# Routed expert results stored in sorted order and gathered by GpSimd, instead of scattered to their tokens

## The reference

```python
x = layernorm(x + self_attention(x))          # 16 heads of 8
x = layernorm(x + cross_attention(x, ctx))    # softmax over the heads
# the feed-forward part, per token:
shared  = gelu(x @ sW1 + sb1) @ sW2 + sb2                     # 512 hidden
weights = softmax(x @ gW + gb)                                # 15 experts
topv, topi = top_k(weights, 3)
routed  = sum over the 3 of  topv * (gelu(x @ rW1[e] + rb1[e]) @ rW2[e] + rb2[e])   # 256 hidden
x = layernorm(shared + routed + x)
```

## Time and profile before

| what | us |
| --- | --- |
| median of 3 runs | 286.7 |
| fastest and slowest of them | 285.6 and 286.87 |
| span of the profiled execution | 319.6 |
| PE, DVE, ACT, POOL busy in it | 241.1, 221.6, 192.2, 179.0 |
| its 62 scatters of results, its 48 scatters of rows | 62.7, 48.0 |

### The profile page before, as it was taken

The page is one execution under the profiler, slowest core; times in us unless marked ns, Lnnn a source line. Parts: engine busy times, 40 slices in busy tenths (PEclk is TensorE's granted clock), DMA queues, the critical chain, the costliest instruction groups (busy, mean ns, idle before and its releaser), DMA issues.

```text
span 319.6 us, 7117 instructions
## 1 busy us (share of the span) xinstructions
PE 241.1 (75%) x2283; PEld 179.8 (56%) x2283; DVE 221.6 (69%) x630; ACT 192.2 (60%) x423; POOL 179.0 (56%) x166
## 2 busy tenths in 40 slices
PE   6989989877988767996761299688868867785970
PEld 3676868655535434452451156586857757674960
DVE  6777999989999998998520497043444434856875
ACT  4697997549976976754470350344554546563665
POOL 6132755330666738985677467135656566665752
PEclk9999999999997998998978589799999999999778
DMA  7672830124000002952211133123132263354462
GB/s 218 217 213 46 181 128 2 37 67 133 2 0 2 0 4 62 378 215 49 86 58 50 44 101 108 41 61 101 53 99 76 75 187 90 91 168 123 150 185 90
DMA packets 38597, 31.89 MB, mean 100 GB/s; under 512 B 12864, under 2 KB 31552, under 8 KB 38432
## 3 DMA queue, kind: packets, MB, share of 16 engines
q1 hardware_dynamic: 34608, 23.90, 26.6%
q0 software_dynamic: 3520, 7.27, 6.7%
q10 hardware_dynamic: 432, 0.27, 0.3%
HBM read 19.95 MB, written 11.47 MB: 98 GB/s over the span
## 4 chain that ended last, share of the span: by engine, by line
PE 44%; DVE 27%; issue 14%; ACT 4%; another core or an unknown queue 4%; POOL 4%; DMA 1%; DVEq 0%; SPq 0%; ACTq 0%
PE psum L994 12%; PE psum L985 9%; PE psum L783 5%; DVE prob_sums L1496 4%; PE psum L763 4%; DVE maxes L1490 3%; PE psum L977 2%; PE psum L568 2%; DVE prob_sums L1410 2%; POOL x_srt L1986 2%; PE psum L585 1%; DMA xT<-x_t 1%; DVE turned_room L1421 1%; DVE maxes L1405 1%
## 5 line engine op out<-in xcount | busy, mean ns | idle before, releaser
L2047 POOL DMA_INDIRECT y_tok<-k_heads,y_rows x62 | 62.7, 1012 | 50.8 <-ACT k_heads L1327 34.4
L1319 ACT ACTIVATE k_heads<-psum,k_heads 128x128 f32<-128x128 f32 x124 | 38.7, 365 | 38.5 <-PE psum L985 33.6
L1986 POOL DMA_INDIRECT x_srt<-v_blocks,slot x48 | 48.0, 1000 | 21.3 <-issue 17.2
L994 PE MATMUL psum<-k_heads 128*128 128x128 f32 x248 | 42.4, 295 | 18.0 <-issue 12.1
L1823 DVE COPY k_heads<-psum 128x128 f32<-128x128 f32 x62 | 17.8, 289 | 48.9 <-PE psum L977 32.7
L994 PEld LDWEIGHTS psum<-k_heads 128*128 128x128 f32 x248 | 34.2, 200 | 21.9 <-issue 15.2
L985 PE MATMUL psum<-k_heads 128*128 128x128 f32 x248 | 40.6, 288 | 5.2 <-DVE k_heads L1823 4.2
L1963 POOL TENSOR_TENSOR k_heads<-k_heads,inv_sums 128x1024 f32<-128x1024 f32 x14 | 27.1, 1939 | 24.0 <-DVE inv_sums L1503 23.9
L985 PEld LDWEIGHTS psum<-k_heads 128*128 128x128 f32 x248 | 33.8, 198 | 8.5 <-DVE k_heads L1823 7.4
L1951 POOL TENSOR_TENSOR probs<-probs,inv_sums 128x512 f32<-128x512 f32 x16 | 16.8, 1050 | 28.9 <-DVE inv_sums L1415 28.7
L1327 ACT ACTIVATE k_heads<-psum,k_heads 128x128 f32<-128x128 f32 x62 | 22.9, 370 | 11.3 <-PE psum L994 9.1
(11 more groups left out here) (191 smaller groups left out, 530.1 us busy)
## 6 DMA issues: line engine op xcount, KB each, us to landing
expert_w<-e_w SPq DMA_DIRECT2D x1, 4369.0 KB
k_heads<-x_srt SPq DMA_DIRECT2D x62, 65.0 KB
q_heads<-y_tok SPq DMA_DIRECT2D x8, 256.0 KB
x_srt<-pad SPq DMA_DIRECT2D x16, 65.0 KB
xT<-x_t SPq DMA_DIRECT2D x4, 256.0 KB, 5.1
ctxT_k<-ctx_k SPq DMA_DIRECT2D x2, 512.0 KB, 5.5
v_scr<-v_rows SPq DMA_DIRECT2D x4, 256.0 KB, 2.8
ctxT_v<-ctx_v SPq DMA_DIRECT2D x2, 512.0 KB, 5.0
```

The source lines that it names most:

```text
L994: mm = pe.matmul(bank[6 + t % 2][:, 0:E], h_tile[:, t % 2, a, :], tile_weights(t)[:, FE + E * a:FE + E * a + E], start=(a == 0), stop=(a = ...
L1319: ins = act.activation(h_tile[:, t % 2, a, :], bank[2 + t % 2][:, P * a:P * a + P], ACT.Gelu, bias=tile_weights(t)[:, EW - 2 + a:EW - 1 + a])
L1986: pool.indirect_dma_start(out=x_srt, out_offset=bass.IndirectOffsetOnAxis(ap=slot[:, n:n + 1], axis=0), in_=payloads[:, g, k, :], in_offse ...
L2047: pool.indirect_dma_start(out=y_tok, out_offset=bass.IndirectOffsetOnAxis(ap=y_rows[:, t:t + 1].bitcast(mybir.dt.uint32), axis=0), in_=y_t ...
```

## The change

A tile's results now go back to the very rows that the tile was read from, by a plain DMA on SP, and POOL gathers them for each token when a chunk's tiles are stored. In detail:

- The table has rows of 128 numbers (`rows_srt`, 34816 rows of 512 B, 17.8 MB). Gates and target rows are no longer in it; the gates stay on the chip in `gate_cols`. The copies of x2 (`payload`) and the padding blocks are gone; POOL's 48 scatters read x2 itself.
- The whole table is set to zero before it is used: `rows_cleared`, eight DMAs on ACT's queue, four before the exponentials of group 11 and four before the first block of queries of cross-attention. POOL waits for all of them (`s_filled`) ahead of its first scatter, SP ahead of the load of the experts' weights.
- In the loop SP, per tile, loads tile t+8 as soon as PE has turned tile t, and stores the results of tile t when ACT has copied them out, now without a scale. Four semaphores (`s_y_stored`) count the stores.
- POOL, after its 48 scatters of rows, loads 16 counts (`t_landed`), and then for each chunk waits for the stores that it needs and gathers the 12 columns of (group, choice) from `rows_srt` into `routed_y`.
- DVE multiplies by the gate and adds in one instruction per group and choice (`added`, `added_last`), at tiles 42 and 57 for chunks 0 and 1, and after the loop for the others. The normalisation of all chunks is on ACT after the loop.

The core of the diff:

```diff
-XW = E + 2
-ROWS = NE * ROOM + P
+ROWS = (NE + 1) * ROOM
+Z = 512
+FILLS = 8
...
+            sp.wait_ge(s_filled, 16 * FILLS)
             sp.dma_start(expert_w[:, :, :], e_w.rearrange("x p f -> p x f")).then_inc(s_expert_w, 16)
...
+            def y_stored(t, rows):
+                sp.wait_ge(s_y_tile, t + 1)
+                if t >= NY:
+                    sp.wait_ge(s_y_stored[t % NY], 16 * (t // NY))
+                sp.dma_start(rows_srt[bass.ds(rows[t // 4][t % 4], P), :], y_tile[:, t % NB, :]).then_inc(s_y_stored[t % NY], 16)
...
             for t in range(NT):
-                if t % 4 == 0:
-                    row_of = nc.values_load_multi_w_load_instructions(
...
+                if t + NB < NT:
+                    if t % 4 == 0:
+                        rows[(t + NB) // 4] = row_of(t + NB)
+                    sp.wait_ge(s_tile_turned, t + 1)
+                    x_loaded(t + NB, rows)
+                y_stored(t, rows)
...
+            def rows_cleared(first, count):
+                act.wait_ge(s_zeros, 1)
+                for i in range(first, first + count):
+                    n = ROWS * E // P // Z
+                    part = rows_srt.rearrange("(p r) e -> p (r e)", p=P).rearrange("p (n z) -> p n z", z=Z)
+                    part = part[:, i * n // FILLS:(i + 1) * n // FILLS, :]
+                    act.dma_start(part, zeros.unsqueeze(1).broadcast_to([P, part.shape[1], Z])).then_inc(s_filled, 16)
...
             k_masked(3)
+            rows_cleared(0, 4)
             exps(11)
...
             k_masked2(2)
+            rows_cleared(4, 4)
             q_masked_first(slice(0, 2))
...
-                        act.wait_ge(s_y_scattered[t % NB], 16 * (t // NB))
-                    act.activation(y_tile[:, t % NB, :], bank[6 + t % 2][:, 0:E], ACT.Copy,
-                                   scale=x_tile[:, t % NB, E:E + 1]).then_inc(s_y_tile, 1)
...
+                        act.wait_ge(s_y_stored[t % NY], 16 * ((t - NB) // NY + 1))
+                    act.copy(y_tile[:, t % NB, :], bank[6 + t % 2][:, 0:E]).then_inc(s_y_tile, 1)
...
+            def added_last(j):
+                g = 4 * (NC - 1) + j
+                dve.wait_ge(s_y_last[j], 16 * TOPK)
+                for k in range(TOPK):
+                    routed(dve.scalar_tensor_tensor(out=acc[:, g, :], in0=routed_y[k][:, g, :], scalar=gate_cols[:, g, k:k + 1],
+                                                    in1=acc[:, g, :], op0=ALU.mult, op1=ALU.add))
+                routed(dve.bn_stats(bn3[:, g, :], acc[:, g, :]))
+                dve.bn_aggr(mean_var3[:, g, :], bn3[:, g, :]).then_inc(s_y_sum, 1)
...
+                    if n == 0:
+                        pool.wait_ge(s_filled, 16 * FILLS)
                     if n % 12 == 0:
                         pool.wait_ge(s_slots, g // 4 + 1)
-                        pool.wait_ge(s_payload_gates, g // 4 + 1)
-                        pool.wait_ge(s_payloads, 2 * (g // 4) + 2)
+                        pool.wait_ge(s_x2, g + 4)
...
-            for t in range(NT):
-                pool.wait_ge(s_y_tile, t + 1)
-                pool.wait_ge(s_y_rows, t // 4 + 1)
-                pool.indirect_dma_start(out=y_tok, out_offset=bass.IndirectOffsetOnAxis(
-                    ap=y_rows[:, t:t + 1].bitcast(mybir.dt.uint32), axis=0),
-                    in_=y_tile[:, t % NB, :], in_offset=None).then_inc(s_y_scattered[t % NB], 16)
+            pool.wait_ge(s_landed, 1)
+            landed = [[pool.value_load(t_landed[0:1, c, k:k + 1], min_val=16 * (max(NE, 4 * TOPK * (c + 1)) // NY),
+                                       max_val=16 * (TABLE // NY)) for k in range(NY)] for c in range(NC)]
+            for c in range(NC):
+                for k in range(NY):
+                    pool.wait_ge(s_y_stored[k], landed[c][k])
+                pool.sem_inc(s_y_through, 1)
+                for n in range(4 * TOPK * c, 4 * TOPK * (c + 1)):
+                    g, k = n // TOPK, n % TOPK
+                    pool.indirect_dma_start(out=routed_y[k][:, g, :], out_offset=None, in_=rows_srt,
+                                            in_offset=bass.IndirectOffsetOnAxis(ap=slot[:, n:n + 1], axis=0)
+                                            ).then_inc(s_y_got[c] if c < NC - 1 else s_y_last[g % 4], 16)
```

More of the change, by code:

```diff
@@ L442, in _ @@
             sp.dma_start(b2_blocks, e_b2.rearrange("p (h a) -> p h a", h=2)).then_inc(s_b2, 16)
-            sp.wait_ge(s_router_ready, 5)
-            sp.dma_start(x_srt[NE * ROOM:ROWS, :], pad[:, :]).then_inc(s_filled, 16)
-            sp.wait_ge(s_ends, 1)
-            for e in range(0, NE, 4):
-                k = min(4, NE - e)
-                ends_of = nc.values_load_multi_w_load_instructions(
-                    ends[0:1, e:e + k], engines=[SP], min_val=0, max_val=NE * ROOM - P,
-                    skip_runtime_bounds_check_because="an expert has room for every token")[1]
-                for j in range(k):
-                    sp.dma_start(x_srt[bass.ds(ends_of[j], P), :], pad[:, :]).then_inc(s_filled, 16)
@@ L490, in _, with row_of @@
-            for g in range(4):
-                sp.wait_ge(s_final_v, g + 1)
-                store(sp, 0, g)
-            for k in range(NB):
-                sp.wait_ge(s_y_scattered[k], landed_all[k])
-            reload_y(sp, NC - 1)
-            for g in range(4):
-                sp.wait_ge(s_final, g + 1)
-                store(sp, 1, g)
-            for g in range(4):
-                sp.wait_ge(s_final, 5 + g)
-                store(sp, NC - 2, g)
-            for g in range(2):
-                sp.wait_ge(s_final_v, 5 + g)
+            def row_of(t):
+                return nc.values_load_multi_w_load_instructions(
+                    tile_of(t, 0), engines=[SP], min_val=0, max_val=ROWS - P,
+                    skip_runtime_bounds_check_because="the table ends at the last tile's row")[1]
@@ L504, in _ @@
+            for g in range(2):
+                sp.wait_ge(s_final_v, g + 1)
                 store(sp, NC - 1, g)
@@ L1147, in exp_logits @@
                 act.activation(route_exp[:, :, :], route_exp[:, :, :], ACT.Exp).then_inc(s_logit_exps, 1)
-            def payload(c):
-                act.wait_ge(s_x2, 4 * c + 4)
-                for k in range(1, TOPK):
-                    act.copy(payloads[:, 4 * c:4 * c + 4, k, 0:E], x2[:, 4 * c:4 * c + 4, :]).then_inc(s_payloads, 1)
             def orT_out(c):
@@ L1277, in _ @@
             u2_out(13)
-            payload(1)
             exp_logits(1)
@@ L1920, in _ @@
                     expert_of = expert_staged(t + 2, expert_of)
+            root_seed(0, NC - 2)
+            for n in range(3):
+                root_newton(0, NC - 2)
+            sum_mean(0, NC - 2)
+            for k in range(TOPK):
+                added(NC - 2, k)
+            sum_stats(NC - 2)
             root_seed(NC - 2, NC - 1)
@@ L1926, in _ @@
             sum_mean(NC - 2, NC - 1)
-            added(NC - 1, 0)
-            added(NC - 1, 1)
-            added(NC - 1, 2)
-            sum_stats(NC - 1)
+            dve.wait_ge(s_acc, NC)
+            for j in range(4):
+                added_last(j)
+            last_stats()
             dve.wait_ge(s_rstd3, 1)
```

199 lines of the change are left out of this document (70 added, 129 removed).

## The result

The changed kernel takes 317.0 us, the kernel before 286.15 (medians of four runs each): 1.111 times as long, interval 1.104 to 1.118. The direction was forecast, the size was not: 296 was said, and 284 to 306.

What follows compares the result with a forecast made beforehand. The prediction took the loop to be bound by indirect transfers on POOL. To the median 286.7 us it added 8.6 for loop and gathers and 1 for work before the loop: 296.3, predicted as 296, range 284 to 306.

Steps and rivals of the forecast that it cites:

- the clear's term: Before the tile loop: eight clearing DMAs issued by ACT, 0.49 us each, net +1 us, between −1 and +3.
- the clear in the way: Rival, before the loop: the clear delays POOL's first scatter by 12 us, about 308, or makes x1 loads late; chance 0.10.
- 9 of slack that costs less: Before the loop: x1 loads made late by the clear have 9 us of slack before POOL needs them.
- About 1.06 per tile, close above PE's 1.0: Tile loop after the change: SP's x load, result store and register loads take about 1.06 us per tile.
- a loop no faster than before: Rival, tile loop: at 1.3 us per tile, chunk 0's gathers start 4.3 later, giving 300.6; chance 0.10, shared with SP-bound loop.
- T0: Start of the tile loop: the moment PE begins the first tile's transposition, 208.85 us in the profile of the kernel before.
- POOL sets the pace: Tile loop of the kernel before: once eight result buffers are full, POOL's scatters set the pace, 1.26 us start to start.
- From there POOL never waits: After chunk 0's gathers start at T0+24.9, POOL runs all 48 gathers without waiting for stores, 1.265 us apart.
- gathers cheaper: Rival, POOL from tile 18 on: gathers start closer than 1.06 us apart, giving 283 to 288; chance 0.17.
- port held, or gathers dear: Rival, POOL's gathers: DVE copies hold the shared port, 16 us more, 311, or gathers at 1.50, 307; chance 0.05.
- the copies add nothing: POOL's transfers in the loop: DVE's SBUF copies beside them lengthen them by 12 ns in the trace, not 438.
- +8.6: From T0 to the end: T0+93.2 after the change against T0+84.6 before, a loss of 8.6 us.

Runs made afterwards that it cites:

- e1: Kernel before plus only the eight clearing DMAs on ACT (17.8 MB, own table) and the two waits for them; 304.13 us, ratio 1.067.
- e4: Changed kernel with a half table (1024 rows per expert, 8.9 MB), cleared by SP behind its x1 loads instead of by ACT; 296.91 us, ratio 1.042.
- e9: Changed kernel with its full 17.8 MB table, the eight clearing DMAs issued by SP behind its x1 loads instead of by ACT; 306.14 us, ratio 1.080.
- e2: Changed kernel clearing the same 17.8 MB at the same places, but in 128 rows of 17.4 KB per DMA; 314.33 us, ratio 1.105.
- e8: Kernel before with every second of POOL's 62 result scatters left out, reloads reading x1 rows instead; 283.17 us, ratio 0.995.
- e6: e4 without the 12 gathers of chunk 0, its sums reading the running sum instead; 296.01 us, ratio 1.038.
- e7: e4 with the 12 gathers of chunk 3 alone, the sums of chunks 0 to 2 reading the running sum instead; 290.69 us, ratio 1.023.

## Why the prediction was wrong

**The step that failed** is the clear's term: "At 0.49 each that is 2.0, and 1.6 after the cover" with its bounds of −1 and +3. The price came from SP's lone loads of 128 KB, where nothing is queued ahead. Behind DMAs of 2048 and 2304 KB an issue took 5.06 and 5.74, and the term was +18.2 (e1; +20.1 by after less e4) and not +1. My upper bound was as wrong as the value: with DMAs seventeen times as large in one queue, the issue could last as long as the transfer, and I did not write that end down. Nor did the term hold anything for the engines behind ACT: PE waited 8.60 and came back at a clock of 0.50.

**The rival "the clear in the way"** (308, 0.10) named the clear, but neither cause at its place. Its first mechanism, a scatter that waits for the clear, is seen only in e9. Its second, late x1 loads, was dismissed with "9 of slack that costs less". For the change as it is the rows bear that out, as far as they go: the loads land 7.4 later (10.4 for 3.0). With the long rows of e2 the bias of the x1 rows is 18.7 late (83.70 to 102.37). That the clear "ends near 97" used the quiet stretch of before; in after a half of the table takes some 27 us, the second starts only at 82.97, and ends near 111.

**The loop** was mis-sized on both sides. "About 1.06 per tile, close above PE's 1.0" took the pace of undisturbed tiles; in after ACT's results come at 212.05 for tile 0 and 279.65 for tile 53, 1.28 per tile, and in e1 1.29. So the rival "a loop no faster than before" is what happened there. The first gather came 26.7 after the last scatter of rows, and 33.6 after T0, where the forecast has 24.9 and this rival 29.2; the wait of 3.60 at tile 8 stood in neither. SP's pace was nearly right, 1.13 per tile where the chain of e4 runs along it, but its stores came later than 2.5 behind the results: tile 53's result is there at 279.65, its store is issued at 283.33. "POOL sets the pace" is half right: POOL has no gap in e1, but taking half of its work away gives 0.5% (e8).

**"From there POOL never waits"** came true in after, but narrowly and by luck. POOL came to chunk 2 at T0+65.5 (274.61, after 0.49 of idle time put down to issue) and not 55, and the store of tile 45, forecast to have landed at T0+53, was issued at 272.07, T0+62.9: both were late by about as much. In e4 POOL waited 2.76 at this place, with twelve gathers fewer 5.14 (e6), so there the gathers of chunk 0 don't count as the prediction has it.

**Right** was the price of a gather, and with it the fall of "gathers cheaper" and of "port held, or gathers dear" at their prices: 993 to 1002 ns, and 61.5 from the first to the last for the 59.5 of the forecast. That the copies add nothing is wrong in detail, since means hid it. In after a scatter that starts 0.06 behind the start of a copy of L1766 took 1.20 (203.07), a gather 0.13 behind one 1.11 (254.38), and two gathers amid DVE's gated sums and a copy 1.28 each (266.09, 267.68), where most took 0.95. Few start so: all 48 gathers together are 2.4 above 48 times 0.95. No run took the copies or the sums away. Right was the form of the loss after T0: gathers that begin only when the tiles are stored cost more than scatters that end with the tiles.

The measured sum, from medians: the clear 18.2 (e1); the last chunk's twelve gathers behind tile 54 in place of a scatter and a reload 6.2 (e7); the gathers of the chunks before it, queued ahead of them, 6.2 (e4 less e7). Together 30.6, of 30.9. That they agree so closely is partly chance, since the runs of before beside e4 and e7 differ by 1.4 (285.91 and 284.52). For the last two the prediction had +8.6; measured are 12.4, or 11.0 if e4 is set against the runs of before beside it, which makes the sum 29.2; with the clear as after less e4, 20.1, it is 31.1. That the +8.6 wasn't further off is luck: counted from T0, after ends at 105.2 (209.15 to 314.3; forecast 93.2, of which the late first gather is 8.7) and before at 90.8 in e1 (209.47 to 300.3; forecast 84.6). Both sums were short, and the errors cancel in part.

The sums of the prediction hold small slips that change nothing: 319.6 less 314.20 is 5.4 and not 5.3, in both sums; and tiles 28, 45 and 54 land at 34.4, 52.4 and 62.0 by its own formula, not at 35, 53 and 63.

What is not settled is the 2.4 by which after's row scatters end later than e1's. Some 1.1 of it is that e1's profiled execution lies 1.9 below its median and after's 0.8; 1.6 is there when ACT is free again (93.54 for 91.95); the cause stays open.

## What to carry to other kernels

Price the issue of a DMA by what already stands in its queue, in rows and in bytes, and not by a lone small DMA: an engine that computes can be held for as long as the transfers ahead take, and what waits behind it can come back slower, as PE did. A transfer with no reader nearby can still be the most expensive part of a change; ask of it whose queue it blocks and whose bytes it delays, and put it on an engine that has nothing to do. When work moves from beside a loop to behind it, count from the last needed tile, and take the loop's pace from all the work in it, in an execution whose span agrees with the runs.

## What the hardware showed

In after ACT's DMA queue took DMAs of 1024 and 1152 rows of 2 KB in 0.40 and 0.61 us and held the engine 5.06 and 5.74 for the next two; with 128 rows of 17.4 KB for nearly the same bytes (e2), four issues took 0.36 to 1.21 each. Long rows have a price of their own: while e2's clear ran at some 410 GB/s, another queue's 256 KB store was 24.42 us under way. In after PE, idle for 8.60, came back at a granted clock of 0.50, and eight products took 1.91 for 1.07. In after an indirect transfer of 128 rows of 512 B mostly takes 0.95 us, and the next starts 0.30 later; beside DVE's copies and sums single ones took up to 1.28.
